# Graph stage of a two-layer graph and expert network: layer-norm statistics split between VectorE and GpSimd, and a second PSUM bank for the mix

## The reference

```
x = x + L0_gnn(layernorm(x), adj)      # gated graph mix
x = x + L0_ffn(layernorm(x))           # 8 experts, the best one for each token
x = x + L1_gnn(layernorm(x), adj)      # the graph stage that is changed here
x = x + L1_ffn(layernorm(x))           # 8 experts, the best two for each token

def L1_gnn(x, adj):
    h = relu(adj @ (x @ Wg0 + bg0))    # for each graph
    h = relu(adj @ (h @ Wg1 + bg1))
    for p in 1..4:                     # windows of p nodes, an LSTM over each,
        h[:, p-1::p] = lstm_p(h)       # its last state put in place of the last node
    return h
```

## Time and profile before

| | |
|---|---|
| median of 3 runs | 1082.03 us (1079.79 to 1086.23) |
| profiled execution, its own time | 1082.45 us |
| its span in the trace | 1080.7 us |
| TensorE busy | 995.4 us (92%) |
| ScalarE busy | 626.1 us (58%) |
| VectorE busy | 602.6 us (56%) |
| GpSimd busy | 489.6 us (45%) |
| TensorE's share of the chain that ended last | 78% |
| graph stage of half 0, first mix to last output mix | 342.68 to 392.38 us |
| graph stage of half 1 begins | 542.06 us |

### The profile page before, as it was taken

One profiled execution on the slowest core, in us unless ns is written; L12 is line 12 of the kernel. 1 busy time (PEld: TensorE's weight loads), 2 busy tenths in 40 slices (PEclk: granted clock), 3 DMA queues, 4 the chain that ended last, 5 costly groups with the idle time before them and its releaser, 6 DMA issues.

```text
span 1080.7 us, 17601 instructions
## 1 busy us (share of the span) xinstructions
PE 995.4 (92%) x5432; PEld 702.9 (65%) x5433; DVE 602.6 (56%) x1832; ACT 626.1 (58%) x1156; POOL 489.6 (45%) x756
## 2 busy tenths in 40 slices
PE   5688987889998989999999999999999999999992
PEld 2333433567776844465478545644899999999992
DVE  6975797611136435655586677444747654444465
ACT  4576865434342467665433776656677776666660
POOL 5661247761371631000022005773543777777762
PEclk9799999899999999999999999999999999999996
DMA  9860001242242221000000000112121232332566
GB/s 284 343 258 1 1 15 48 70 122 86 77 126 59 77 78 64 0 1 1 0 1 1 1 1 33 53 48 68 39 61 48 74 97 74 93 95 73 198 226 199
DMA packets 79876, 86.29 MB, mean 80 GB/s; under 512 B 10114, under 2 KB 65970, under 8 KB 79026
## 3 DMA queue, kind: packets, MB, share of 16 engines
q1 hardware_dynamic: 67250, 59.28, 17.4%
q0 software_dynamic: 12544, 25.98, 7.5%
HBM read 40.64 MB, written 44.58 MB: 79 GB/s over the span
## 4 chain that ended last, share of the span: by engine, by line
PE 78%; DVE 13%; ACT 4%; issue 2%; DMA 1%; POOL 1%; ACTq 0%; DVEq 0%; SPq 0%; POOLq 0%
PE bank L1380 17%; PE bank L1407 15%; PE bank L1387 9%; PE bank L1417 8%; PE bank L1256 5%; PE bank L1131 5%; PE bank L1296 2%; PE bank L1324 2%; PE bank L1157 2%; PE bank L1097 2%; PE bank L1313 1%; PE bank L1285 1%; PE bank L1397 1%; DVE sb_R L1507 1%; PE bank L1305 1%
## 5 line engine op out<-in xcount | busy, mean ns | idle before, releaser
L1380 PE MATMUL bank<-sb_R,sb_wih_sb 128*128 128x512 f32 (+2 forms) x504 | 197.9, 543 | 1.5 <-issue 1.2
L956 ACT ACTIVATE sb_R<-bank,sb_lb_sb 128x512 f32<-128x512 f32 (+2 forms) x252 | 153.5, 634 | 72.7 <-PE bank L1387 64.0
L703 POOL DMA_INDIRECT expert_out<-sb_R,sb_slot_row x136 | 134.3, 988 | 86.6 <-ACT sb_R L979 44.9
L1380 PEld LDWEIGHTS bank<-sb_R,sb_wih_sb 128*128 128x128 f32 x504 | 95.3, 190 | 96.8 <-issue 75.7
L2193 DVE TENSOR_TENSOR sb_R<-sb_R,bank 114x384 f32<-114x384 f32 x136 | 75.3, 554 | 136.6 <-ACT sb_R L1013 90.6
L1013 ACT ACTIVATE sb_R<-bank 114x384 f32<-114x384 f32 x136 | 66.8, 491 | 101.8 <-PE bank L1407 98.1
L1417 PE MATMUL bank<-sb_BIG,sb_R 114*128 x816 | 113.9, 276 | 0.5 <-DVE sb_R L2122 0.5
L1387 PE MATMUL bank<-sb_R,sb_whh_sb 128*128 128x512 f32 (+2 forms) x288 | 111.1, 529 | 0.0
L606 POOL TENSOR_TENSOR sb_ln_p<-sb_ST 128x8 f32<-128x8 f32 (+2 forms) x14 | 3.4, 240 | 237.4 <-DVE sb_ST L1622 160.9
L678 POOL DMA_INDIRECT expert_in<-sb_R,sb_dest_i x64 | 66.4, 1037 | 84.4 <-DVE sb_dest_i L1732 63.0
L1417 PEld LDWEIGHTS bank<-sb_BIG,sb_R 114*128 114x128 f32 x816 | 101.8, 192 | 0.7 <-issue 0.7
(11 more groups left out here) (303 smaller groups left out, 1691.6 us busy)
## 6 DMA issues: line engine op xcount, KB each, us to landing
sb_XS<-expert_in SPq DMA_DIRECT2D x17, 528.0 KB, 4.0
expert_in<-sb_R SPq DMA_DIRECT2D x17, 512.0 KB, 6.4
sb_R<-expert_out SPq DMA_DIRECT2D x6, 1024.0 KB, 8.4
sorted_in<-sb_R SPq DMA_DIRECT2D x9, 512.0 KB, 5.5
sb_XS<-sorted_in SPq DMA_DIRECT2D x18, 256.0 KB, 3.1
sorted_out<-sb_R SPq DMA_DIRECT2D x18, 256.0 KB, 2.4
sb_X<-x SPq DMA_DIRECT2D x8, 512.0 KB, 7.5
out<-sb_X SPq DMA_DIRECT2D x6, 512.0 KB, 4.5
```

Source lines behind the costliest of these rows:

```text
L703: pool.indirect_dma_start(out=expert_out, out_offset=bass.IndirectOffsetOnAxis(ap=slot_row[:, i:i + 1], axis=0), in_=yd[i // 8 % RING][:, ...
L956: act.activation(gb[s][k][:, 0:c], bank[4 * s + k][:, 0:c], funcs[k], bias=lb_sb[:, (p - 1) * GATES + k:(p - 1) * GATES + k + 1]).then_inc ...
L1380: mm = pe.matmul(bank[4 * s + k][:, 0:c].rearrange("p (w b) -> p w b", b=GH), wih_sb[:, p - 1, k * P:(k + 1) * P], xin, start=True, stop=( ...
```

## The change

- In the expert stage, VectorE finishes the statistics of tiles 0 to 23 (SOON = 24) behind group 15's tiles, where before it finished those of all 32 tiles behind group 16's. The scalings of steps 0 and 1 of half 0 follow there, ahead of the evictions of groups 16 and 17.
- The statistics of tiles 24 to 31 are finished by GpSimd, between its gathers of tiles 24 to 31 and those of 32 to 63. It waits there for b3_t of 32 tiles, and gives b3_rstd. VectorE waits for b3_rstd ahead of the scaling of step 6 in half 0.
- Mix 1 of each half goes to bank 3, and no longer waits for the copy of mix 0. `g_mixed` reads it from there.
- `b3_finish` loses its argument; the second half's statistics stay as they are.

```diff
+        SOON = 3 * NH // 4
+        def mix_bank(i):
+            return bank[3] if i == 1 else bank[0]
...
             for lo, hi, done in GATHERS:
                 gather(lo, hi, done)
+                if hi == NH:
+                    pool.wait_ge(b3_t, NH)
+                    ln_finish(SOON, NH, False, b3_rstd)
...
-                act.activation(axt[i % 2], bank[0][:, :], ACT.Copy).then_inc(c1_axc, 1)
+                act.activation(axt[i % 2], mix_bank(i)[:, :], ACT.Copy).then_inc(c1_axc, 1)
...
             def g_mix(half, i):
                 n = half * NGH + i
                 pe.wait_ge(c1_xn, n + 1)
-                if n > 0:
+                if n > 0 and i != 1:
                     pe.wait_ge(c1_axc, n)
                 for b in range(2):
                     for m in range(MC):
-                        mm = pe.matmul(bank[0][:, b * N:(b + 1) * N], xn[i % 2][:, MC * b + m, :], adj_sb[:, m, :],
+                        mm = pe.matmul(mix_bank(i)[:, b * N:(b + 1) * N], xn[i % 2][:, MC * b + m, :], adj_sb[:, m, :],
...
-            def b3_finish(half):
-                dve.wait_ge(b3_t, (half + 1) * NH)
-                ln_finish(half * NH, (half + 1) * NH)
+            def b3_finish():
+                dve.wait_ge(b3_t, 2 * NH)
+                ln_finish(NH, 2 * NH)
...
             def g_norm(half, i):
                 n = half * NGH + i
                 if n >= 2:
                     dve.wait_ge(c1_ax, n - 1)
+                if half == 0 and 4 * i == SOON:
+                    dve.wait_ge(b3_rstd, 1)
...
             def b2_dve(g, k, u, first, last):
-                if isinstance(g, int) and g == NB2 - 1:
-                    g_norm(0, 0)
-                    g_norm(0, 1)
...
                 if 2 <= ahead_of_end <= 5:
                     for t in range((5 - ahead_of_end) * NH // 4, (6 - ahead_of_end) * NH // 4):
                         b3_tile(t)
-                if ahead_of_end == 2:
-                    b3_finish(0)
+                if ahead_of_end == 3:
+                    dve.wait_ge(b3_t, SOON)
+                    ln_finish(0, SOON)
+                    g_norm(0, 0)
+                    g_norm(0, 1)
```

More of the change, by code:

```diff
@@ L309, in build @@
         yb = [view(R3, u * BANK, 4, D) for u in range(2)]
-        b3_x, b3_t = sem("b3_x"), sem("b3_t")
+        b3_x, b3_t, b3_rstd = sem("b3_x"), sem("b3_t"), sem("b3_rstd")
+        SOON = 3 * NH // 4
+        def mix_bank(i):
+            return bank[3] if i == 1 else bank[0]
         c1_xn, c1_ax, c1_axc, c1_h, c1_hb, c1_hr, c1_z, c1_zc, c1_g, c1_f = (
@@ L2113, in _ @@
                     if half == 0 and n == NL - 3:
-                        b3_finish(1)
+                        b3_finish()
             def d2_rows_out(i):
```

## The result

| | before | after |
|---|---|---|
| median of 5 runs | 1081.75 us (1079.79 to 1086.23) | 1074.11 us (1070.57 to 1076.06) |
| ratio to before | | 0.9915, 95% interval 0.9891 to 0.9939 |
| profiled execution, its own time | 1082.45 us | 1070.57 us |
| its span | 1080.7 us | 1068.8 us |

The changed kernel is faster by 0.85%, 6.6 to 11.8 us by the interval. The direction was forecast, and the forecast size of 6.9 us lies in this interval. The median, 1074.11 us, lies in the range that was given, 1072.8 to 1079.0.

What follows compares the result with a forecast made beforehand. TensorE was taken as the bound, with 78% of the chain that ended last. 2.76 + 1.96 + 0.84 in half 0 and 1.3 in half 1 made 6.9 us, forecast 1075.3 us, own range 1073.3 to 1077, full range 1072.8 to 1079.0.

Steps and rivals of the forecast that it cites:

- Theory A: Follow-up forecast: the change is worth what its steps say, 5.5 to 7.5 us; the surplus is chance in the front.
- theory B: Follow-up forecast: the change itself is worth 9 us or more, ratio 0.9915 or less.
- Idle time of 2.76 us: Half 0, TensorE ahead of the first mix: the wait for the first scaling goes, worth 2.76 us.
- Clock in the first mix, 1.96 us: Half 0: without the gap the clock does not fall, the first mix takes 1.73 instead of 3.69 us.
- Second mix, half 0: With bank 3 it starts without waiting for ScalarE's copy of the first mix, worth 0.84 us.
- Half 1: The second mix waits for its own scaling and not the first mix's copy: 1.3 us won, bounds 0 and 2.06.
- GpSimd's part at no cost: Statistics of tiles 24 to 31, 3.7 us, fit GpSimd's idle time ahead of the second half's gathers: cost 0.
- VectorE's slack of 1.1 us: Half 0: the third scaling is due at 344.3 us and comes at 343.2.
- Rival (b): VectorE becomes the bound in half 0, each 1 us beyond its slack costing 1 us: 1078 us, chance 13%.
- the sign that the first copy waits for the residual sum: Half 0: ScalarE's copy of the first mix waiting for VectorE's residual sum would show the prediction wrong.
- the 0.76 us of half 1's upper bound: Half 1's second mix: the margin between the 1.3 us taken and the upper bound of 2.06 us.
- The terms of the sum: 2.76 + 1.96 + 0.84 us in half 0 and 1.3 us in half 1, together 6.9 us.

Runs made afterwards that it cites:

- last eight on VectorE: The changed kernel, with the statistics of tiles 24 to 31 finished on VectorE behind group 16's tiles instead of on GpSimd; ratio to before 0.9944.
- half 1 scalings sooner: The changed kernel, with the second half's statistics and its first two scalings one LSTM step sooner; ratio to before 0.9913, median 1075.82 us.
- before, gap filled (6): The kernel before, with 6 unused products on TensorE between the last group 17 product and the first mix; ratio to before 0.9986.
- the experiment that was to take falls away from the front: The changed kernel with half 1's scalings one LSTM step sooner, plus 3 and 4 filling products at two places in the front; ratio to before 0.9989.
- the fillers: Two runs of the kernel before with 6 or 3 unused products on TensorE ahead of the first mix; ratios to before 0.9986 and 0.9992.

## Why the prediction was right in its steps and short in its range

To set the front apart I cut each profile of the quick chips where the last group 17 products end. All numbers are us. The estimate adds up (1 - granted clock) x 2 us over the stretches of 2 us from 0 to 336 us; the moment in the next column is read from the timeline, the columns behind it are differences of starts and ends, and the last is the span less the moment.

| profile | time lost to the clock up to 336 us, estimate | last group 17 product ends | from there to third mix | half 1, first to third mix | from that product to the span's end |
|---|---|---|---|---|---|
| before | 17.1 | 339.91 | 10.03 | 7.51 | 740.8 |
| before, one more profile | 17.1 | 339.07 | 9.93 | 7.49 | 740.8 |
| after | 10.2 | 335.53 | 4.24 | 6.22 | 733.3 |
| last eight on VectorE | 10.3 | 335.54 | 6.58 | 6.21 | 735.4 |
| half 1 scalings sooner | 20.5 | 344.74 | 4.24 | 5.49 | 732.3 |
| before, gap filled (6) | 20.5 | 344.34 | 10.46 | 9.18 | 742.7 |

Behind that moment the two profiles of before agree within 0.1 us, and the change is worth 740.8 - 733.3 = 7.5 us. Of the changed kernel there is one profile on a quick chip.

Ahead of it the moment moves from 335.5 to 344.7 us, over kernels whose work on TensorE is alike up to there, and it goes with the clock. The two profiles that lost 10 us have it at 335.5, the two that lost 17 us at 339.1 and 339.9, the two that lost 20.5 us at 344.3 and 344.7. The last pair is one kernel of either kind. The whole times go the same way: of the 23 runs of before on the second chip, those with a mean granted clock of 0.978 or more took 1080.1 to 1080.8 us, and those with 0.971 or less 1084.5 to 1088.3 us. That the falls set the moment is not shown by it: the experiment that was to take falls away from the front missed. On the slow chips the moment lies between 352.5 and 357.6 us (without the run with fillers in the front) and does not follow the estimate; there the three profiles with the statistics moved have it no sooner (354.2, 355.1 and 357.6) than the three without (352.5, 352.9 and 355.2).

The slow chips bear the gain out over both graph stages, but not to the end. From the last group 17 product to the first LSTM product of half 1, before takes 263.3 and 263.2 us on the quick chips and 266.4 on the first slow one, and the changed kernel 256.2, and 259.1 and 259.2 on the two slow ones: 7.0 to 7.1 us on quick chips and 7.3 to 7.4 on slow ones. From that product to the span's end, though, the changed kernel takes 796.6 us on one slow chip and 804.9 on the other, 8.3 us apart. So the cut resolves the change there only up to the second LSTM stage.

Theory A fits all of this: of the two later ratios of the changed kernel one, 0.9934, is in its range and the other, 0.9953, shows if anything less gain, and its interval leaves theory B out. The first comparison had 4.4 us of the front in its two profiles.

Point by point:

- **Idle time of 2.76 us**: right, gone in every profile with the statistics moved.
- **Clock in the first mix, 1.96 us**: right in size on quick chips and in cause (the fillers show the cause). On the first slow chip the fall went on over the second mix (3.75 us), and before was 12.82 us instead of 10.03; the sum had no case for that. The reason that I gave for its not coming back was wrong in its rows: I had read 2.06 us as an idle time that has no fall behind it. It had one in two other executions, and 2.70 and 3.29 us had none. What the change does is to leave no idle time at all ahead of the first mix.
- **Second mix, half 0**: right. Half 0 as a whole 10.03 - 4.24 = 5.79 us, 5.6 forecast.
- **Half 1**: 1.29 us, 1.3 forecast. Where the clock falls behind the 2.06 us, as in two other profiles with the mix in bank 0, that stretch takes some 1.7 us more (9.17 and 9.18 against 7.50), and I had no term for that.
- **A remainder of 0.4 us** in half 1's LSTM stage: TensorE has an idle time of 0.33 us ahead of 666.44 in before that the changed kernel doesn't have. I did not follow it, so its cause stays open.
- **GpSimd's part at no cost, VectorE's slack of 1.1 us**: both right, by 4.24 with it and 6.58 without it.
- **Rival (b)** came true on both slow chips, at its price of one for one, 1.5 us, by evictions that start late there and not by GpSimd, and with it the sign that the first copy waits for the residual sum.
- **The step that failed** is the one from the sum to the measured time. The prediction takes everything ahead of the last group 17 product as equal in the two kernels, that is, it puts the front at nothing, and it gives no reason. That moment moved over 9 us from execution to execution (335.5 to 344.7), with the clock falls of the front, and 4.4 us of it are in the two profiles compared. Its range knows only the 0.76 us of half 1's upper bound and a median that "moves by about 1.5 us", where the interval of five runs against five is 2.6 us to either side.
- **The low end of the range** does not follow from its own numbers either. 1075.3 less 1.5 is 1073.8 and not 1073.3, and less the 0.76 us it is 1073.0; 1073.3 less 0.76 is 1072.5. The 1072.8 is neither.
- **The terms of the sum** come to 5.8 + 1.3 us against 5.6 + 1.3, and with the 0.4 us that were not foreseen to 7.5 against 6.9. From 1082.03 us, 7.5 us less and 2.6 us for the spread, the range would have begun near 1071.9, and the 1072.6 us of the ratio would lie in it.
- **That the ratio says 9.2 us** and not 7.5 is, by its interval of 6.6 to 11.8 us, by the medians' 7.6 us and by the later ratios of 0.9934 and 0.9953, not shown to be more than chance. Whether a value came out just inside the range (the median, by 1.3 us) or just outside (by the ratio, 0.2 us) was luck: both distances are smaller than the 2.6 us.

## What to carry to other kernels

An idle time of TensorE cost its own length here and, when the clock fell behind it, 0.7 to 0.8 times as much again in what followed (1.96 us behind 2.76, 1.7 behind 2.06); look at the granted clock behind each idle time before pricing it, and take no length that you saw once without a fall as safe. Where the front of a kernel spreads by more than the change is worth, cut the profiles at an instruction that both kernels have ahead of the change: here that turned 6.6 to 11.8 us into 7.5. Repeat the profiles of both kernels before trusting the cut: on the slow chips two profiles of one kernel still differed by 8.3 us behind it, and only a nearer end to the stretch told the change. A slack of 1 us on a helper engine is real on one chip and may be gone on the next, so give the shortest one its margin.

## What the runs showed of the hardware

- The same kernel took 1083.7 us on one chip and 1160.6 and 1167.4 on two others, 7 to 8% more. On the first slow chip matmuls of a group have the same length (3.73 us), but the eviction of group 15 starts 4.6 us behind its products instead of 0.15, and ScalarE's gelus start late at the same moment. I have not settled why.
- Whether the clock fell behind an idle time differed from execution to execution: behind 2.05 to 2.06 us it fell in two profiles (0.71 and 0.79) and not in others, behind 2.70 and 3.29 us it did not fall in one, behind 2.75 to 3.06 us ahead of the first mix it fell in all four. The end of the front moved by 9 us along with such falls.
- VectorE's scaling beside GpSimd's arithmetic kept its 1.11 us, and one GpSimd instruction of nine went from 0.20 to 0.28 us.
- The Trainium skill (GPSIMD Engine Reference, Specifications) says that GpSimd shares its SBUF interfaces with VectorE, with contention when VectorE runs in a two-port mode or has two SBUF inputs. The 0.28 us would agree with that, on GpSimd's side alone; in which mode the scaling runs no trace here shows.
